# Attention scores as two products of rounded halves, four banks of queries and keys, and another order of side work

## The chip, the cores and the metric

The kernel runs on one core of a Trainium2 chip. The metric is the device time of one execution in microseconds (us), lower is better; it is read as the median of several runs. The engines are named as in the profile: PE (TensorE, matmuls; PEld are its weight loads), DVE (VectorE), ACT (ScalarE), POOL (GpSimd) and SP (SyncE, here only a queue of DMAs).

## What is computed

A batch of 8 sequences of 256 tokens with 128 features goes through four residual steps. The first one, which the change touches, is an attention with 16 heads, 16 features per head for queries and keys and 64 for values:

```
q, k, v = l2norm(q), l2norm(k), l2norm(v)
sim = einsum('bhid,bhjd->bhij', q, k)
attn = square(relu(sim))
out = tanh_norm(einsum('bhij,bhjd->bhid', attn, v))
x = x + out @ Wout
x = x + mixture_of_experts(layernorm(x))     # 32 experts of 64, top 8, and a shared one
x = x + sum_d softmax(W x + b)[d] * shifted(x, d)
x = x + mixture_of_experts(layernorm(x))     # the same weights
```

All tensors are float32, and the output must agree with a float32 reference. The norms of q, k and v are divided out behind the products (in the values' scales and in the output factors), so that the scores are made of unnormalised q and k.

## The kernel before

Everything is written out by hand: each engine has its own instruction list, and semaphores order them. There are two stages.

**Attention, `for b in range(B)`.** A batch b has four groups (slots of four heads), g = 0 to 3, numbered i = 4b + g over all. For each group PE makes `score(i)` (four banks S0), ACT `relu(i)`, DVE `squares(i)` (tile aT), PE `attend(i)` (bank O0) and ACT `keep_output(i)`. Between these stands other work. With n = b + 1 there is the preparation of the next batch: `transpose_tokens`, `pairs(n, t)` (q and k by token, for the norms), `values(n, t, k)` and `group(n, j)`, which makes q and k with features in rows, as score needs them. With q = b - 1 and r = b - 2 there is the finishing of earlier batches: `norms`, `transpose_norms`, `output_factors` (DVE), `transpose_factors`, `spread_factors`, `scale_output` (DVE, tile OTs) and `project(r, it)`, whose sum `add_attention` (DVE) adds to X.

**Three banks in rotation.** All of PE's side results go to banks 5, 6 and 7 in turn (W2, W0, W1). `attention_turns` writes the order of the jobs; a job can only start when the job three places ahead of it in that order has been read out (its `free_of` semaphore). The names of the jobs are xT (tokens), qk (pairs), v (values), g (groups), nb and nt (norms), ft and F (factors), y (project). In `group` a half bank is filled by one triple of products: x and the weights are each the sum of a rounded half and a low half (fp32r: one pass, where float32 takes two passes per recorded matmul and two records), and `split3` makes high by high, high by low and low by high. ACT's `keep_group` copies a group bank to the tile qk in float32, and that copy frees the bank.

**Expert weights.** The expert weights come in 32 pieces through six staging tiles (`STAGES`): SP loads a piece, ACT rounds it (`weight_high`, tile wfh), DVE makes the low half (`weight_low`, tile wfl). One piece goes in each of the 32 group steps, and the low halves of a batch are made in the batch behind it. SP's queue is in order, and a load of a piece waits for the low half made six pieces before.

**Experts, `for u in range(NU)`.** Eight units of 17 pairs each. PE makes `gate_up` and, four pairs later, `down`; ACT makes Silu and the rounded half, DVE two products, POOL the low half. In unit 0 the last batches' outputs are finished at fixed pairs p.

The order in which DVE works within a batch (before):

```
squares(NG * b + 3)
if more:
    value_norms(n, 1)
    clear_norms(n, 1)
if b:
    output_factors(q)
squares(NG * b + 4)
if n + 1 < B:
    tokens_low(n + 1)
```

Of the kernel before, what the change touches and what calls it, by code (L numbers as in the profile page):

```python
# [39 lines left out]
NQ = NG // 2 + 1  # L40
WQ_G, WK_G = (0, 1, 4, 5), (2, 3)
# [10 lines left out]
STAGES = 6  # L52
PC = WF // PIECES

# [28 lines left out]
def attention_turns(turns):  # L83
# [11 lines left out]
    for b in range(B):  # L95
        n, q, r = b + 1, b - 1, b - 2
        order += late(r, ("F", r, 2), ("F", r, 3)) + ([("pt", 0)] if b == B - 1 else [])
        order += coming(n, ("qk", n, 0), ("qk", n, 1), ("v", n, 0, 0), ("v", n, 0, 1)) + late(q, ("nb", q))
# [5 lines left out]
        order += coming(n, ("g", n, 0), ("g", n, 1), ("g", n, 2))  # L104
# [36 lines left out]

def up_banks():
# [16 lines left out]
def hybrid_layer(nc, x_in, wa_in, wo_in, wb_in, bb_in, gw_in, wf_in, sd_in, band, wdram, out):  # L159
# [4 lines left out]
    with ExitStack() as ctx:  # L164
# [9 lines left out]
        rowf = sb("rowf", [P, 1])  # L174
        sel = sb("sel", [P, 2, P], F32R)
# [36 lines left out]
        wTs = sb("wTs", [P, P])  # L212

# [3 lines left out]
        ld = Sems(ctx, nc, "in_x0 in_x in_wv0 in_wv1 in_wq in_wp in_wo in_wf0 in_wf1 in_wf2 in_wf3 in_wf4 in_wf5 in_sd in_gw in_wb in_bb zeroed")  # L217
        cs = Sems(ctx, nc, "id0 id half floors rid ind0 ind rm rf sel fpad zero sel1 sdz wah wal wph wpl wfh wfl sdh sdl")
        A = Sems(ctx, nc, "stats mv ve rstd xn xTh vraw sqv n2v n2q nm nm_v rr vi vc0 vc vp S relu a av Oc sqO "
# [20 lines left out]
        with ExitStack() as att:  # L240
# [10 lines left out]
            qk = ab("qk", [P, NQ, 2 * L])  # L251
# [143 lines left out]
        def _(pool):  # L395
# [126 lines left out]
            for u in range(NU):  # L522
                for p in range(NE if u < NU - 1 else NE - 1):
# [3 lines left out]
                    if u == 0 and p == 5:  # L527
                        last_output_norms(1)
                    if u == 0 and p == 6:
                        last_output_scales()  # L530
                    if p == (3 if u else 4) and u + 1 < NU:
# [7 lines left out]
        def _(act):  # L539
# [5 lines left out]

            first_weights_high(0)
# [111 lines left out]
            keep_group(0, 0)  # L658
            keep_group(0, 1)
            relu(0)  # L660
            tokens_high(1)
            for j in range(2, NQ):
                keep_group(0, j)
            for b in range(B):
# [14 lines left out]
                weight_high(NG * b)  # L679
# [7 lines left out]
                weight_high(NG * b + 1)  # L687
# [6 lines left out]
                if more:  # L694
                    square_values(n, 1)
                    keep_group(n, 0)
                    keep_group(n, 1)
                keep_output(NG * b + 2)
                if more:
                    keep_group(n, 2)  # L700
# [4 lines left out]
                weight_high(NG * b + 2)  # L705
# [4 lines left out]
                if last:  # L710
                    prep_normalise(1, range(CT // 2, CT))
# [4 lines left out]
                weight_high(NG * b + 3)  # L716
# [69 lines left out]
            for u in range(NU):  # L786
                first = u == 0
                for p in range(NP):
# [7 lines left out]
                    if first:  # L796
                        if p == 1:
                            keep_norms(B - 1)
                        if p == 8:
                            tanh_norms(B - 1)  # L800
                        if p == 11:
# [35 lines left out]
        def _(dve):  # L837
# [5 lines left out]
            dve.wait_ge(cs("rf"), 1)  # L843
            for m in range(HG):
# [38 lines left out]
            def clear_norms(n, t):  # L883
# [4 lines left out]
                v_.reciprocal(rr[:, n % 3, t, :], nm[:, n % 3, t, 0:2 * H]).then_inc(A("rr"), 1)  # L888

# [154 lines left out]
            normalise(1)  # L1044
            squares(0)
            tokens_low(1)
            first_scale_values()
            dve.wait_ge(cs("sel1"), 2)
            dve.wait_ge(cs("fpad"), 1)
            for b in range(B):  # L1050
# [20 lines left out]
                if b:  # L1071
                    if not last:
                        for k in range(NG * q, NG * b):
# [11 lines left out]
                if r >= 0:  # L1085
                    add_attention(r, 0)
                squares(NG * b + 3)
                if more:
                    value_norms(n, 1)
# [3 lines left out]

                squares(NG * b + 4)
                if n + 1 < B:
# [7 lines left out]
                if last:  # L1103
                    for k in range(NG * q, NG * b + 3):
# [76 lines left out]
            weight_low(NS - 1)  # L1181
            for u in range(NU):
                first = u == 0
                for p in range(NP):
# [3 lines left out]
                    if first:  # L1188
                        if p == 3:
                            gather_norms(B - 1)  # L1190
                        if p == 8:
                            output_factors(B - 1)
                        if p == 12:
                            scale_output(B - 1, 0)
                            scale_output(B - 1, 1)
                        if p == 14:
# [4 lines left out]
                        if p == 16:  # L1201
# [490 lines left out]
```

## Time and profile before

| | before |
|---|---|
| median of 3 runs | 548.19 us (547.99 to 548.92) |
| profiled execution | 546.98 us, of which the span is 545.2 us |
| instructions | 10298 |
| PE busy | 526.1 us (96%) |
| DVE busy | 421.7 us (77%) |
| ACT busy | 371.2 us (68%) |
| POOL busy | 332.5 us (61%) |
| granted TensorE clock | 0.999 of full speed |
| attention stage | from the start to about 215 us, some 26 us per batch |

The span is the time from the first to the last instruction of the profiled execution; its own time is 1.8 us more. Busy times are sums of recorded spans and say nothing of who waits for whom. That is read from the timeline of each engine: a start, a length, and in brackets the idle time ahead of an instruction and what ended it. Matmuls are pipelined, so that the next one starts before the one ahead is recorded as ended.

### The profile page before, as it was taken

What the parts mean: (1) busy time and instruction counts of PE and PEld (TensorE: products, weight loads), DVE (VectorE), ACT (ScalarE), POOL (GpSimd) and SP (SyncE); (2) the same over time, 40 slices, a digit from 0 to 9 for tenths busy, and PEclk for the clock granted to TensorE, in tenths of its full rate; (3) what the DMA queues carried; (4) which work ended last, traced back from release to release, by engine and by line L of the source; (5) the groups of instructions that cost most, each with busy time, mean ns of one, the idle gap of its engine ahead of it and who ended that gap; (6) DMA issues with size and microseconds to landing.
All of it is one profiled execution on the core that took longest, in us unless ns stands there. A gap on an engine that the chain in (4) does not pass through costs nothing.

```text
span 545.2 us, 10298 instructions
## 1 busy us (share of the span) xinstructions
PE 526.1 (96%) x3322; PEld 394.0 (72%) x3322; DVE 421.7 (77%) x1004; ACT 371.2 (68%) x682; POOL 332.5 (61%) x282
## 2 busy tenths in 40 slices
PE   7899899999999999998999999999999999999997
PEld 6565667676666666776778778778778877788884
DVE  5877888788979687669679679779778778777765
ACT  5697877686778876654555965965965965755654
POOL 6754938475865664484566656656655655666562
PEclk9999999999999999999999999999999999999999
DMA  7401010101010100850490940850860870761930
GB/s 222 131 2 31 1 32 1 32 0 32 1 31 1 31 2 21 189 122 1 107 208 7 222 116 5 207 132 6 197 141 7 194 163 5 181 149 42 220 74 20
DMA packets 37254, 44.77 MB, mean 82 GB/s; under 512 B 5840, under 2 KB 20304, under 8 KB 37200
## 3 DMA queue, kind: packets, MB, share of 16 engines
q1 hardware_dynamic: 32512, 42.40, 33.3%
q10 hardware_dynamic: 4688, 1.71, 1.3%
q8 instruction: 27, 0.44, 0.4%
q14 instruction: 27, 0.22, 0.2%
HBM read 40.94 MB, written 3.15 MB: 81 GB/s over the span
## 4 chain that ended last, share of the span: by engine, by line
PE 29%; POOL 12%; issue 9%; DVE 1%; DMA 1%; ACT 0%; POOLq 0%; DVEq 0%; SPq 0%; ACTq 0%
PE PS L1247 28%; POOL hl L519 10%; DMA wbc<-w_dram 1%; POOL mrstd L510 1%; POOL rstd L463 1%; DVE OTs L931 0%; PE PS L1534 0%; PE PS L1368 0%; DVE PS L1115 0%; DVE wsel L991 0%; POOL fxl L470 0%; PE PS L1555 0%; DVE hb L1120 0%; POOL mve L507 0%; DVE hl L1233 0%
## 5 line engine op out<-in xcount | busy, mean ns | idle before, releaser
L519 POOL TENSOR_TENSOR hl<-hb,hh 128x512 fp32r<-128x512 f32 x127 | 164.5, 1296 | 128.7 <-ACT hh L737 125.5
L730 ACT ACTIVATE sil<-PS 128x512 f32<-128x512 f32 (+1 forms) x136 | 80.8, 595 | 78.8 <-PE PS L1247 77.6
L1115 DVE TENSOR_TENSOR PS<-sil,PS 128x512 f32<-128x512 f32 x128 | 88.3, 690 | 53.0 <-PE PS L1247 32.3
L1247 PE MATMUL PS<-fxh,wfh 128*128 128x512 f32 x264 | 105.1, 398 | 2.5 <-DVE hb L1120 2.5
L737 ACT ACTIVATE hh<-hb 128x512 fp32r<-128x512 f32 x128 | 80.3, 627 | 35.1 <-DVE hb L1120 34.3
L1247 PE MATMUL PS<-fxl,wfh 128*128 128x512 f32 x264 | 104.2, 395 | 0.0
L1247 PE MATMUL PS<-fxh,wfl 128*128 128x512 f32 x264 | 103.8, 393 | 0.0
L1120 DVE TENSOR_TENSOR hb<-PS,wbc 128x512 f32<-128x512 f32 x128 | 88.5, 691 | 13.7 <-DMA wbc<-w_dram 6.4
L896 DVE SCALAR_TENSOR_TENSOR aT<-PS,rl 128x1024 f32<-128x1024 f32 x64 | 75.2, 1217 | 15.0 <-ACT rl L583 14.7
L583 ACT ACTIVATE rl<-PS 128x1024 f32<-128x1024 f32 x64 | 62.9, 1051 | 18.7 <-PE PS L1247 18.7
L438 POOL TENSOR_TENSOR sr<-n2o,half 128x32 f32<-128x32 f32 x7 | 37.9, 5413 | 44.3 <-DVE n2o L903 44.3
L1247 PE MATMUL PS<-aT,v 128*64 128x256 f32 x512 | 62.3, 385 | 0.6 <-POOL v L434 0.6
L1247 PEld LDWEIGHTS PS<-fxh,wfh 128*128 128x128 f32 x264 | 49.6, 188 | 15.8 <-DVE hb L1120 3.4
L1247 PEld LDWEIGHTS PS<-fxh,wfl 128*128 128x128 f32 x264 | 49.6, 188 | 11.9
L1247 PEld LDWEIGHTS PS<-fxl,wfh 128*128 128x128 f32 x264 | 49.6, 188 | 11.4
L1247 PE MATMUL PS<-hh,wfh 128*128 128x512 f32 x128 | 54.2, 424 | 1.0 <-DVE hl L1233 0.6
L1247 PE MATMUL PS<-hh,wfl 128*128 128x512 f32 x128 | 50.6, 396 | 0.0
L1247 PE MATMUL PS<-hl,wfh 128*128 128x512 f32 x128 | 50.5, 394 | 0.0
L1247 PEld LDWEIGHTS PS<-aT,v 128*64 128x64 f32 x512 | 34.0, 136 | 22.6 <-issue 5.6
L425 POOL TENSOR_TENSOR vi<-nm,half 128x16 f32<-128x16 f32 x14 | 40.5, 2894 | 9.8 <-DVE rr L888 9.8
L1247 PE MATMUL PS<-qk 32*128 32x256 f32 x512 | 37.5, 398 | 4.0 <-DVE aT L896 3.3
L1247 PEld LDWEIGHTS PS<-qk 32*128 32x128 f32 x512 | 24.4, 184 | 11.2 <-issue 7.1
(186 smaller groups left out, 899.6 us busy)
## 6 DMA issues: line engine op xcount, KB each, us to landing
wbc<-w_dram SPq DMA_DIRECT2D x48, 512.0 KB, 11.5
wbc<-w_dram SPq DMA_DIRECT2D x32, 128.0 KB, 3.0
wbc<-w_dram SPq DMA_DIRECT2D x16, 256.0 KB, 4.2
wfs<-wf_dram SPq DMA_DIRECT2D x32, 98.0 KB, 2.3
band_dram<-zero SPq DMA_DIRECT2D x16, 80.0 KB, 1.7
band<-band_dram ACTq DMA_DIRECT2D x4, 320.0 KB, 3.0
X<-x_dram SPq DMA_DIRECT2D x1, 896.0 KB, 8.0
Osb<-wa_dram SPq DMA_DIRECT2D x3, 256.0 KB, 3.8
```

The lines of the kernel that those rows point to most:

```text
L425: g.tensor_tensor(vi[:, t, :], nm[:, n % 3, t, 2 * H:3 * H], half[:, 1:2].to_broadcast([P, H]), ALU.pow).then_inc(A("vi"), 1)
L438: g.tensor_tensor(sr[:, :, :], n2o[:, :, :], half[:, 0:1].unsqueeze(2).to_broadcast([P, 2, H]), ALU.pow).then_inc(A("sr"), 1)
L463: g.tensor_tensor(rstd[:, :], ve[:, :], half[:, 1:2].to_broadcast([P, CT]), ALU.pow).then_inc(F("p_rstd"), 1)
L510: g.tensor_tensor(mrstd[:, :], mve[:, :], half[:, 1:2].to_broadcast([P, CT]), ALU.pow).then_inc(M("m_rstd"), 1)
L519: g.tensor_tensor(hl[:, n % RING, :], hb[:, n % RING, :], hh[:, n % RING, :].bitcast(F32), ALU.subtract).then_inc(F("hl"), 1)
L583: s.activation(rl[:, f, :, :], PS[:, S0 + 2 * f:S0 + 2 * f + 2, :], ACT.Relu).then_inc(A("relu"), 1)
L730: s.activation(sil[0:rows, n % 2, :], PS[0:rows, G0 + n % 2, :], ACT.Silu).then_inc(F("silu"), 1)
L737: s.activation(hh[:, n % RING, :], hb[:, n % RING, :], ACT.Copy).then_inc(F("hh"), 1)
L896: v_.scalar_tensor_tensor(aT[:, i % 2, 2 * f:2 * f + 2, :], PS[:, S0 + 2 * f:S0 + 2 * f + 2, :], 0.0, rl[:, f, :, :], ALU.max, ALU.mult).t ...
L1115: v_.tensor_tensor(PS[:, bank, :], sil[:, n % 2, :], PS[:, bank, :], ALU.mult).then_inc(F("t"), 1)
L1120: v_.tensor_tensor(hb[:, n % RING, :], PS[:, bank, :], wbc[u % 2][:, p, :], ALU.mult).then_inc(F("h"), 1)
L1247: return nc.tensor.matmul(o, w, m, start=start, stop=stop)
```

## The change

The float32 score product is replaced. `group` now makes four banks per batch: j = 0 holds the keys of groups 0 and 1, j = 1 their queries, j = 2 and 3 the same for groups 2 and 3. In each slot of 32 rows the 16 features of a head stand twice (the weights are laid out so). `group_high` (ACT) rounds a bank to fp32r, keys to kst, queries to qh. `group_low` (DVE) follows on the same bank and frees it: for queries it writes ql = q - qh; for keys it turns only the lower 16 rows of each slot into k - kh, by a column `low` that is 0 or -1. `score` makes two fp32r products that add up in the bank, kst by qh and kst by ql, which give (kh + kl)(qh + ql). Score waits for the two banks of its pair of groups to be free.

Beside that, `norms` stands ahead of the first `attend` of a batch; the pieces of the expert weights follow a table (none in batches 0 and 7, four in 1 and 6, six in 2 to 5) with seven stages; the last batches' outputs are finished one or two pairs earlier in unit 0; the filling transposes at the start of batch 0 are 4, not 10; and a Silu of one column stands first in ACT's list.

```
-NQ = NG // 2 + 1
-WQ_G, WK_G = (0, 1, 4, 5), (2, 3)
+NQ = NG
-STAGES = 6
+STAGES = 7
+PIECES_IN_SLOTS = ((0, 0, 0, 0), (1, 1, 1, 1), (1, 2, 1, 2), (1, 2, 1, 2), (1, 2, 1, 2), (1, 2, 1, 2), (1, 1, 1, 1), (0, 0, 0, 0))
...
-        order += coming(n, ("qk", n, 0), ("qk", n, 1), ("v", n, 0, 0), ("v", n, 0, 1)) + late(q, ("nb", q))
+        order += coming(n, ("qk", n, 0), ("qk", n, 1)) + late(q, ("nb", q)) + coming(n, ("v", n, 0, 0), ("v", n, 0, 1))
...
-        order += coming(n, ("g", n, 0), ("g", n, 1), ("g", n, 2))
+        order += [("g", n, j) for j in range(NQ)]
         order += coming(n + 1, ("xT", n + 1)) + late(q, ("ft", q)) + late(r, ("y", r, 1))
...
+            act.wait_ge(cs("half"), 2)
+            s.activation(unread[:, :], half[:, 0:1], ACT.Silu)
...
-            def keep_group(n, j):
+            def group_high(n, j):
                 act.wait_ge(*full("g", n, j))
-                after(act, A("S"), 2 * (NG * (n - 1) + (2 if j == 0 else NG)))
-                s.activation(qk[:, j, :], PS[:, bank_of("g", n, j), :], ACT.Copy).then_inc(free_of("g", n, j), 1)
+                after(act, A("S"), 2 * (NG * (n - 1) + (2 if j < 2 else NG)))
+                high = (qh if j % 2 else kst)[:, j // 2, :]
+                s.activation(high, PS[:, bank_of("g", n, j), :], ACT.Copy).then_inc(A("gh"), 1)
...
+            def group_low(n, j):
+                dve.wait_ge(A("gh"), NQ * n + j + 1)
+                x, k = PS[:, bank_of("g", n, j), :], j // 2
+                if j % 2:
+                    v_.tensor_tensor(ql[:, k, :], x, qh[:, k, :].bitcast(F32), ALU.subtract).then_inc(free_of("g", n, j), 1)
+                else:
+                    v_.scalar_tensor_tensor(kst[:, k, :], kst[:, k, :].bitcast(F32), low[:, 0:1], x, ALU.mult,
+                                            ALU.add).then_inc(free_of("g", n, j), 1)
...
                 squares(NG * b + 3)
                 if more:
+                    group_low(n, 0)
+                    group_low(n, 1)
                     value_norms(n, 1)
                     clear_norms(n, 1)
                 if b:
                     output_factors(q)
 
+                if more:
+                    group_low(n, 2)
                 squares(NG * b + 4)
+                if more:
+                    group_low(n, 3)
...
-                pe.wait_ge(*freed("g", b, jq))
-                pe.wait_ge(*freed("g", b, 1))
+                c = g % 2 * L
+                pe.wait_ge(*freed("g", b, g // 2 * 2))
+                pe.wait_ge(*freed("g", b, g // 2 * 2 + 1))
                 after(pe, A("a"), 2 * i)
                 for jt in range(2):
-                    for s in range(HG):
-                        rows = slice(SLOT * s, SLOT * (s + 1))
-                        last = mm(PS[:, S0 + s, jt * L:(jt + 1) * L], qk[rows, 1, k0 + jt * P:k0 + (jt + 1) * P],
-                                  qk[rows, jq, q0:q0 + L], True, True)
...
+                    for part, queries in enumerate((qh, ql)):
+                        for s in range(HG):
+                            rows = slice(SLOT * s, SLOT * (s + 1))
+                            last = mm(PS[:, S0 + s, jt * L:(jt + 1) * L], kst[rows, g // 2, c + jt * P:c + (jt + 1) * P],
+                                      queries[rows, g // 2, c:c + L], part == 0, part == 1)
...
-                    fill_idle(10 if b == 0 else 8, "qk", n, 0)
+                    fill_idle(4 if b == 0 else 8, "qk", n, 0)
...
+                if b:
+                    norms(q)
                 attend(NG * b)
...
                     group(n, 2)
+                    group(n, 3)
```

**Where DVE's instructions go.** Before, in batch 2, DVE's list from the squares of the third group (aT) to the low half of the next tokens (xTl) reads as follows; nmx to Fpad are `output_factors`:

```order
L896 SCALAR_TENSOR_TENSOR aT<-PS,rl 128x1024 [waits av,relu] x2
L875 TENSOR_REDUCE n<-sqv 128x16 [waits sqv]
L886 TENSOR_REDUCE nm<-n 128x48 [waits n2q,n2v]
L888 RECIPROCAL rr<-nm 128x32 [waits nm]
L908 TENSOR_REDUCE nmx<-nn 128x32 [waits n]
L910 RECIPROCAL rec<-nmx 128x32 [waits nmx]
L912 TENSOR_TENSOR f<-rec,rr 128x32 [waits rec]
L915 TENSOR_TENSOR ff<-f,th 128x32 [waits th,f1]
L922 CAST Fpad<-ff 128x8x4 [waits full6,ff]
L924 TENSOR_TENSOR Fpad<-ff,Fpad 128x8x4 [waits fhi]
L896 SCALAR_TENSOR_TENSOR aT<-PS,rl 128x1024 [waits av,relu] x2
L868 TENSOR_TENSOR xTl<-PS,xTh 128x256 [waits xTh]
```

In the changed kernel the same place begins with two of the four new instructions (kst and ql are what `group_low` writes),

```order
L933 SCALAR_TENSOR_TENSOR aT<-PS,rl 128x1024 [waits av,relu] x2
L924 SCALAR_TENSOR_TENSOR kst<-kst,low,PS 128x512 [waits gh]
L922 TENSOR_TENSOR ql<-PS,qh 128x512 [waits gh]
L903 TENSOR_REDUCE n<-sqv 128x16 [waits sqv]
L914 TENSOR_REDUCE nm<-n 128x48 [waits n2q,n2v]
```

and ends, behind the same `output_factors`, with the other two around the squares of the fourth:

```order
L961 TENSOR_TENSOR Fpad<-ff,Fpad 128x8x4 [waits fhi]
L924 SCALAR_TENSOR_TENSOR kst<-kst,low,PS 128x512 [waits gh]
L933 SCALAR_TENSOR_TENSOR aT<-PS,rl 128x1024 [waits av,relu] x2
L922 TENSOR_TENSOR ql<-PS,qh 128x512 [waits gh]
L896 TENSOR_TENSOR xTl<-PS,xTh 128x256 [waits xTh]
```

So three new instructions stand between the two squares, and the fourth, which frees the last group bank, stands behind the second squares.

**What PE waits for.** Before, PE's list in batch 3 from the third group bank (first row) over the last score (qk), the next tokens (xnA) and the factors' transposition (Fpad) to the second `project` (wout) is this; the third group bank and `project` share bank 5 (free5):

```order
L1247 MATMUL PS<-xTh,wah 128x256 [waits free5]
...
L1247 MATMUL PS<-qk 128x256 [waits a,free7,free6]
L1247 MATMUL PS<-qk 128x256 x7
L1267 MATMUL PS<-ident,xnA 128x128 [waits free6,xn]
L1267 MATMUL PS<-ident,xnA 128x128
...
L1340 MATMUL PS<-ident,Fpad 128x128 [waits free7,f]
L1340 MATMUL PS<-ident,Fpad 128x128
L1247 MATMUL PS<-wout,OTs 128x128 [waits free5,free7,free6]
```

In the changed kernel, same batch, the fourth group bank (first row) and `project` (last row) share bank 5, with nothing on that bank in between:

```order
L1297 MATMUL PS<-xTh,wah 128x256 [waits free5]
...
L1297 MATMUL PS<-qh,kst 128x256 [waits a,free6,free5]
...
L1317 MATMUL PS<-ident,xnA 128x128 [waits free6,xn]
...
L1391 MATMUL PS<-ident,Fpad 128x128 [waits free7,f]
...
L1297 MATMUL PS<-wout,OTs 128x128 [waits free7,free6,free5]
```

Before, that bank was read out by one ACT copy; now `project` stands behind the `group_low` that DVE has behind its squares.

**The start.** Before, DVE's list ahead of the first squares is

```order
L875 TENSOR_REDUCE n<-sqv 128x16 [waits sqv]
L1016 TENSOR_REDUCE nm<-n 128x16 [waits n2v]
L863 TENSOR_SCALAR xnA<-X,mvA,rsA 128x128 [waits full6,rstd]
L863 TENSOR_SCALAR xnA<-X,mvA,rsA 128x128
L896 SCALAR_TENSOR_TENSOR aT<-PS,rl 128x1024 [waits relu] x2
```

and in the changed kernel

```order
L903 TENSOR_REDUCE n<-sqv 128x16 [waits sqv]
L1053 TENSOR_REDUCE nm<-n 128x16 [waits n2v]
L891 TENSOR_SCALAR xnA<-X,mvA,rsA 128x128 [waits full6,rstd]
L891 TENSOR_SCALAR xnA<-X,mvA,rsA 128x128
L924 SCALAR_TENSOR_TENSOR kst<-kst,low,PS 128x512 [waits gh,low]
L922 TENSOR_TENSOR ql<-PS,qh 128x512 [waits gh]
L933 SCALAR_TENSOR_TENSOR aT<-PS,rl 128x1024 [waits relu] x2
```

The first score, on PE, now stands behind the first kst and ql of this list.

## Rows read from the trace of the kernel before

**Rows 1.** The page: busy time, and the granted clock in 40 slices.

```profile
PE 526.1 (96%) x3322; PEld 394.0 (72%) x3322; DVE 421.7 (77%) x1004; ACT 371.2 (68%) x682; POOL 332.5 (61%) x282
PEclk9999999999999999999999999999999999999999
```

**Rows 2.** Busy time in batch 4: window, then PE, PEld, DVE, ACT, POOL.

```profile
120.00:146.00 26.00, 25.77 (x228) 17.72 (x230) 22.20 (x49) 20.02 (x36) 17.16 (x13) 1.00 0.07 17
```

**Rows 3.** PE timeline of batch 4: start, length, line, tiles, count.

```profile
118.52 0.39 PE L1247 MATMUL PS<-FT,sel 32*128 32x256 f32 x2
133.48 1.15 PE L1247 MATMUL PS<-qk 32*128 32x256 f32 x16
...
134.90 0.28 PE L1247 MATMUL PS<-xTh,wal 128*128 128x256 f32 x1
...
135.97 0.28 PE L1247 MATMUL PS<-xTh,wal 128*128 128x256 f32 x1
...
138.97 1.15 PE L1247 MATMUL PS<-qk 32*128 32x256 f32 x16
140.05 0.44 PE L1267 MATMUL PS<-ident,xnA 128*128 128x128 f32 x2
...
142.57 1.95 PE L1247 MATMUL PS<-wout,OTs 128*128 128x128 f32 x16
144.45 0.39 PE L1247 MATMUL PS<-FT,sel 32*128 32x256 f32 x2
```

**Rows 4.** DVE timeline of batch 4.

```profile
119.06 2.63 DVE L931 TENSOR_TENSOR OTs<-Osb,PS 128x512 f32<-128x512 f32 x4
...
135.18 0.38 DVE L954 BATCH_NORM_AGGREGATE mv<-stats 128x2 f32<-128x6 f32 x4
...
135.72 2.36 DVE L896 SCALAR_TENSOR_TENSOR aT<-PS,rl 128x1024 f32<-128x1024 f32 x2
...
141.30 2.36 DVE L896 SCALAR_TENSOR_TENSOR aT<-PS,rl 128x1024 f32<-128x1024 f32 x2
143.57 0.41 DVE L868 TENSOR_TENSOR xTl<-PS,xTh 128x256 fp32r<-128x256 f32 x1
```

**Rows 5.** ACT timeline of batch 4: the third and fourth relu.

```profile
134.66 1.94 ACT L583 ACTIVATE rl<-PS 128x1024 f32<-128x1024 f32 x2 [0.94 <-PE PS L1247]
...
140.19 1.99 ACT L583 ACTIVATE rl<-PS 128x1024 f32<-128x1024 f32 x2
```

**Rows 6.** Tile qk from 113.0 to 114.2 us: durations in ns, first and last start.

```profile
L1247 PEld LDWEIGHTS PS<-qk x16: 181/184/185, 113.0 to 113.6; 32*128 32x128 f32 x16
L1247 PE MATMUL PS<-qk x16: 374/374/478, 113.0 to 113.8; 32*128 32x256 f32 x16
```

**Rows 7.** PE and DVE timelines of the start and of batches 1 and 2.

```profile
15.19 1.15 PE L1247 MATMUL PS<-qk 32*128 32x256 f32 x16 [0.61 <-ACT qk L575]
16.81 0.59 DVE L863 TENSOR_SCALAR xnA<-X,mvA,rsA 128x128 f32<-128x128 f32 x2
17.42 2.36 DVE L896 SCALAR_TENSOR_TENSOR aT<-PS,rl 128x1024 f32<-128x1024 f32 x2
...
19.92 1.15 PE L1247 MATMUL PS<-qk 32*128 32x256 f32 x16 [0.93 <-DVE aT L896]
...
41.91 1.15 PE L1247 MATMUL PS<-qk 32*128 32x256 f32 x16 [0.53 <-DVE aT L896]
...
65.83 1.10 PE L1247 MATMUL PS<-qk 32*128 32x256 f32 x13 [0.76 <-DVE aT L896]
```

**Rows 8.** ACT, PE and SP timelines where the experts begin.

```profile
215.10 1.82 SPq L361 DMA_DIRECT2D w_dram<-wTs  x4
216.29 0.37 ACT L613 ACTIVATE wfh<-wfs 128x196 fp32r<-128x196 f32 x1 [4.09 <-DMA wfs<-wf_dram]
...
217.74 0.51 PE L1247 MATMUL PS<-FT,sel 32*128 32x256 f32 x4 [1.27 <-ACT FT L605]
...
218.93 1.28 ACT L730 ACT_TABLE_LOAD   x1
...
223.22 0.50 PE L1247 MATMUL PS<-fxh,wfh 128*128 128x512 f32 x1 [1.08 <-DVE hb L1120]
...
247.85 0.50 PE L1247 MATMUL PS<-fxh,wfh 128*128 128x512 f32 x1 [1.42 <-DVE hb L1120]
```

More of the change, by code:

```diff
@@ L139, in expert_turns, with pieces_in @@
             turns.add(MB, "pc", u + 1)
+def pieces_in(b, slots=range(NG)):
+    first = sum(sum(PIECES_IN_SLOTS[c]) for c in range(b))
+    a = first + sum(PIECES_IN_SLOTS[b][:slots[0]])
+    return range(a, a + sum(PIECES_IN_SLOTS[b][k] for k in slots))
 def up_banks():
@@ L174, in hybrid_layer @@
         rowf = sb("rowf", [P, 1])
+        rowh = sb("rowh", [P, 1], I32)
+        rowg = sb("rowg", [P, 1])
+        low = sb("low", [P, 1])
         sel = sb("sel", [P, 2, P], F32R)
@@ L678, in _ @@
                     keep_norms(q)
-                weight_high(NG * b)
+                for k in pieces_in(b, [0]):
+                    weight_high(k)
                 relu(NG * b + 2)
@@ L686, in _ @@
                 keep_output(NG * b + 1)
-                weight_high(NG * b + 1)
+                for k in pieces_in(b, [1]):
+                    weight_high(k)
                 if b == B - 2:
@@ L704, in _ @@
                     tanh_norms(q)
-                weight_high(NG * b + 2)
+                for k in pieces_in(b, [2]):
+                    weight_high(k)
+                if last:
+                    prep_normalise(1, range(CT // 2, CT))
                 relu(NG * b + 4)
@@ L715, in _ @@
                     keep_factors(q)
-                weight_high(NG * b + 3)
+                for k in pieces_in(b, [3]):
+                    weight_high(k)
                 if b == 0:
@@ L843, in _ @@
             dve.wait_ge(cs("rf"), 1)
+            v_.tensor_scalar(rowh[:, :], rowid[:, :], DK, None, ALU.bitwise_and).then_inc(cs("rh"), 1)
+            dve.wait_ge(cs("rh"), 1)
+            v_.tensor_copy(rowg[:, :], rowh[:, :]).then_inc(cs("rg"), 1)
+            dve.wait_ge(cs("rg"), 1)
+            v_.tensor_scalar(low[:, :], rowg[:, :], -1.0 / DK, None, ALU.mult).then_inc(cs("low"), 1)
             for m in range(HG):
@@ L1044, in _ @@
             normalise(1)
+            dve.wait_ge(cs("low"), 1)
+            group_low(0, 0)
+            group_low(0, 1)
             squares(0)
             tokens_low(1)
+            group_low(0, 2)
+            group_low(0, 3)
             first_scale_values()
@@ L1072, in _ @@
                     if not last:
-                        for k in range(NG * q, NG * b):
+                        for k in pieces_in(q, [0, 1]):
                             weight_low(k)
@@ L1086, in _ @@
                     add_attention(r, 0)
+                if b and not last:
+                    for k in pieces_in(q, [2, 3]):
+                        weight_low(k)
                 squares(NG * b + 3)
                 if more:
+                    group_low(n, 0)
+                    group_low(n, 1)
                     value_norms(n, 1)
@@ L1103, in _ @@
                 if last:
-                    for k in range(NG * q, NG * b + 3):
+                    for k in pieces_in(q):
                         weight_low(k)
@@ L1440, in _ @@
                     values(n, 0, 1)
-                if b:
-                    norms(q)
                 score(NG * b + 2)
```

62 lines of the change are left out of this document (32 added, 30 removed).

## Prediction, made before the changed kernel ran

> **What bounds the kernel now.** I read the page first: PE is busy 526.1 of 545.2 us at the full clock in all 40 slices [rows 1], and the reader is to see that only PE time, or a new wait of PE, can count. Then busy time by batch: in 26 us of batch 4 PE works 25.77, DVE 22.20, ACT 20.02 [rows 2]. So PE bounds a batch, but DVE has under 4 us to spare. Then the timelines of PE and DVE side by side in batch 4, for where those 4 us lie. PE's batch runs from 118.52 to 144.45, 25.93 us [rows 3]. DVE's spare time is not where the change adds work: from the squares at 135.72 over the squares at 141.30 to their end at 143.57 DVE has no idle bracket [rows 4]. Last the start and the passage to the experts, the two places where PE does wait: for DVE at the start [rows 7], and at 217.74, 223.22 and 247.85 [rows 8].
>
> **The score product.** A score's 16 recorded matmuls start in 0.8 us, four waves for four row groups, and PE goes on at 140.05 where the score began at 138.97: 1.08 us [rows 3, 6]. A wave is 256 columns in two passes; with the next start 1.08 us later I put 4 x 0.213 = 0.85 for the waves (my reading of the 0.8 us from first to last start) and 0.23 fixed. The new one has four waves of one pass. In `group` fp32r matmuls of 256 columns start (135.97 - 134.90) / 9 = 0.119 us apart, with a new weight load each [rows 3]. So a score takes 0.48 + 0.23 = 0.71, 0.37 less; 32 of them, 12 us of PE. Bounds: nothing, if 16 weight loads took as long as the old product; 0.43 (half of 0.85) at best. I take 0.37, since the row with loads is the nearest.
>
> The Trainium skill speaks against it: TensorE: Matmul & The Clock Gate, section LDWEIGHTS, says that a load takes its columns by 1.2 GHz, no matter how few rows. For 128 columns that is an estimate of 0.107 us, and 16 in a line would be 1.7 us, a score slower than now. The row has 16 loads starting within 0.6 us [rows 6], so loads of four row groups run side by side; the trace decides.
>
> **The fourth group bank.** Six more matmuls at 0.119: 0.72 us of PE per batch, 8 times; one more ACT copy (0.55). PE's own work per batch falls by 4 x 0.37 - 0.72 = 0.76 us.
>
> **The four new DVE instructions.** The trace has no instruction like them on group banks; the nearest reads a PSUM bank and a tile of 512 columns: four in 2.63 us, 0.66 each [rows 4]. I take 0.64; bounds 0.55 and 0.70. That is 2.6 us per batch, and six weight pieces for four add 0.6: 22.2 becomes 25.4 of DVE work against 25.2 of PE. This already leaves no room, and the order decides more than the sum.
>
> **The walk from the third score of a batch (time 0).** Before: relu starts at 1.18 [rows 5], the squares at 2.24, the fourth squares at 7.82 to 10.09, `project` at 9.09 (142.57 - 133.48) [rows 3, 4]. After: the score ends 0.37 earlier, so squares at 1.87. Between the two squares three `group_low` come in: 7.82 - 0.37 + 3 x 0.64 = 9.37; the squares' 2.27 take it to 11.64, the fourth `group_low` to 12.3. `project` shares its bank with the fourth group bank, so it waits for that. PE itself would be there at 9.09 - 2 x 0.37 + 0.72 = 9.07. A stall of **3.2 us**, where there was none. The relu is no help: 6.71 less 0.37 plus one more copy 0.55, so it is there before the squares. Queued behind `project` on PE are the spreading of factors and the next batch's first score; DVE waits in turn for the factors and then has its idle time there.
>
> The first half of the batch (118.52 to 133.48, 14.96) can give back little: two scores, 0.74, of which some 0.45 goes to a bank of the values that now waits for ACT's copy of the norms, and the pairs still wait for DVE's second product. I take 0.3 saved. Per batch: +3.2 - 0.02 - 0.3 = **+2.9**. This holds for batches 2 to 5. In batch 4 the statistics that end at 135.56 [rows 4] leave 0.2 us ahead of the squares, where two or three weight pieces at 0.3 now come too: +0.6. Sum of the four: +12.2.
>
> **Batch 6** has no tokens to come, so the rotation gives `project` the third bank, and only the router's logits wait for the fourth: +1.0. **Batch 7** has three scores and no group: PE could save 1.1; DVE holds the first one, I take -0.8.
>
> **The start.** The first score began at 15.19 behind an ACT copy; now it stands behind DVE's normalisation, which ends at 17.40, and two `group_low`: 18.7 [rows 7]. Its squares ran 17.42 to 19.69; now relu comes 1.7 behind the score's start, so 20.4 to 22.7; the low half of tokens 0.4 and a third `group_low` 0.64 let the filling go at 23.75, and the second score comes at 24.2 for 19.92, +4.3. In batch 0 ACT has no weight pieces and PE's later waits absorb 1.5 of it. Batch 1 meets the same chain as above, with the filling and the next score in place of `project` behind the fourth bank (65.83 before [rows 7]): +2.2. Sum for the first two batches **+5.0**, bounds +3 and +7.
>
> **The passage to the experts.** ACT waited 4.09 us there for a weight piece that hung in SP's queue, and PE 1.27 us for factors behind it; SP's store of the expert factors (215.10) hung there too; the Silu table took 1.28 at 218.93 [rows 8]. With the pieces done before batch 7 and the table loaded at the start, where ACT waits for its first DMA, PE's wait of 1.27 goes. That of 1.08 at 223.22 stays in part, since the pair behind it needs DVE's first hidden product, which stands behind DVE's four factor products. With the table's delay out I take -1.7. The wait of 1.42 at 247.85 stood behind `output_factors` and the router in one pair; they are apart now: -1.4. Bounds of the two: -1 and -4. The seventh stage and `norms` ahead of `attend` I cost at nothing: the load is hidden by a batch's distance, and `norms` only changes place.
>
> **Sum.** +5.0 + 12.2 + 1.0 - 0.8 - 3.1 = +14.3 on the profiled 546.98: 561.3. The median of the runs shown is 1.2 more, so **562.4** on it.
>
> **Rivals.**
> 1. *The chain is looser (half the stall).* If DVE's instructions overlap more than the rows show, or the third score comes earlier against DVE, the stall is 1 to 2 us a batch and the start +2 to +3. At 1.5: (1.5 - 0.3) x 4 + 0.6 + 2.5 + 0.5 - 3.9 = +4.5, 552.7. For it: DVE's idle time in a batch is real; against it: it lies elsewhere.
> 2. *PE stays the bound (faster).* One mechanism: `group_low` of the fourth bank is off PE's path, since what stands on that bank does not hold `project`. Then seven batches save 0.76 and batch 7 0.8, the passage 3.1, and the start costs what its chain costs, about +2: 548.2 - 5.3 - 0.8 - 3.1 + 2 = 541.0. It decides once the fourth bank is free 9.1 us behind the third score. Four free instructions would bring it to 12.3 - 2.6 = 9.7, so a low price for them alone is not enough; the squares ahead of it would have to end earlier too. The order of the banks speaks against it.
> 3. *The clock falls in the stalls.* The trace has no idle time of PE above 1.5 us behind the start and no slice below the full clock [rows 1]. A wait of 3.2 us per batch and one of 4 us at the start are new. If the 3 us of work behind each ran at half speed: 5 x 3 = 15 us more, 577. The page named above says in its section on oscillation that idle gaps send the clock back to half; by it the sum would be this one.
> 4. *The new product saves nothing* (loads in line): +0.37 x 32 less what the stalls cover (the scores ahead of a stall of DVE): some +6, 568.
>
> **Chances.** The walk as it stands, with its error, 553 to 567: 0.56. Rival 1: 0.12. Rival 2: 0.17. Rival 3: 0.06. Rival 4: 0.05. Within 0.2%, which is about what a measurement of this kernel can tell from no change, 0.04. So faster 0.17, same 0.04, slower 0.79. The predicted time is that of the walk. The range goes from 542, into rival 2, to 570, over rival 4; left out are the lower half of rival 2 and rival 3. The walk's own range is 553 to 567.
>
> **What the profile will show.** Right: in batches 2 to 5 a PE wait of about 3 us at wout, with DVE's ql as what ended it; a batch of 28.8 us; DVE without idle time from the third squares to ql; scores 0.7 us apart from what follows; the second score near 24 us; ACT's wait for a weight piece gone. Wrong: a batch under 26 us, or PE waits that end on ACT; new DVE instructions under 0.5 us; a score slot still of 1.08; or a granted clock below 0.98.

## The result, and the profile after

The changed kernel takes 574.88 us (median of 4 runs, 572.89 to 575.23) against 548.56 us (4 runs, 547.99 to 550.62): a ratio of 1.047, 95% interval 1.044 to 1.050. It is slower. The forecast of slower was right; the time of 562.4 us is 12.5 us short, and the range (542 to 570) does not hold the result. The profiled execution took 574.87 us, of which the span is 573.1, 27.9 more than before.

The page of the kernel after, busy time and the granted clock in 40 slices:

```profile
PE 533.8 (93%) x3364; PEld 403.8 (70%) x3364; DVE 441.5 (77%) x1039; ACT 375.7 (66%) x690; POOL 332.1 (58%) x282
PEclk9799999898989899999999999999999999999999
```

Against [rows 1] PE is busy 7.7 us *more*, though its scores are shorter, and the clock row, flat before, has dents in slice 2 and in every second one from 8 to 14. A page that shows more busy time for less work says: look at the clock. Next the batches 2 to 6 by windows (window, its length, then PE, PEld, DVE, ACT, POOL, and the clock as a share of full speed):

```profile
74.81:105.57 30.76, 26.43 (x235) 18.94 (x234) 23.18 (x43) 21.12 (x38) 16.60 (x10) 0.96 0.06 15
105.57:135.91 30.34, 26.53 (x235) 19.06 (x234) 24.02 (x46) 21.05 (x38) 16.60 (x10) 0.95 0.09 21
135.91:166.59 30.68, 26.90 (x235) 19.23 (x234) 24.95 (x54) 21.09 (x38) 18.35 (x14) 0.95 0.08 21
166.59:196.56 29.97, 26.36 (x235) 18.90 (x235) 24.02 (x46) 22.49 (x42) 16.60 (x10) 0.96 0.09 21
196.56:226.12 29.56, 27.88 (x245) 19.82 (x244) 23.97 (x48) 21.29 (x37) 15.97 (x9) 0.91 0.05 12
```

A batch of 25.93 [rows 3] has become 30.0 to 30.8. PE timeline of batch 3, from the third score to the next batch:

```profile
120.55 0.39 PE L1297 MATMUL PS<-qh,kst 32*128 32x256 f32 x4
...
121.22 0.39 PE L1297 MATMUL PS<-xTh,wah 128*128 128x256 f32 x1
...
127.74 1.68 PE L1297 MATMUL PS<-aT,v 128*64 128x256 f32 x14
130.04 0.41 PE L1391 MATMUL PS<-ident,Fpad 128*128 128x128 f32 x2 [0.62 <-DVE kst L924]
132.90 3.06 PE L1297 MATMUL PS<-wout,OTs 128*128 128x128 f32 x16 [2.45 <-DVE ql L922]
135.89 0.58 PE L1297 MATMUL PS<-FT,sel 32*128 32x256 f32 x2
...
137.56 0.50 PE L1297 MATMUL PS<-FT,sel 32*128 32x256 f32 x4 [0.17 <-DVE OTs L968]
```

Three things are to be seen. The score's slot is 121.22 - 120.55 = 0.67 us, for 1.08 before [rows 3]. Ahead of `project` PE stands still twice, 0.62 and 2.45, together 3.07, both ended by an instruction of `group_low`. And `project` itself now takes 3.06 us for 16 matmuls that took 1.95. DVE's timeline of the same stretch says why PE waits:

```profile
122.38 2.36 DVE L933 SCALAR_TENSOR_TENSOR aT<-PS,rl 128x1024 f32<-128x1024 f32 x2 [0.62 <-ACT rl L600]
124.73 0.75 DVE L924 SCALAR_TENSOR_TENSOR kst<-kst,low,PS 128x512 fp32r<-128x512 f32 x1
125.39 0.68 DVE L922 TENSOR_TENSOR ql<-PS,qh 128x512 fp32r<-128x512 f32 x1
125.99 1.21 DVE L903 TENSOR_REDUCE n<-sqv 128x16 f32<-128x1024 f32 x1
...
129.16 0.74 DVE L924 SCALAR_TENSOR_TENSOR kst<-kst,low,PS 128x512 fp32r<-128x512 f32 x1
129.81 2.35 DVE L933 SCALAR_TENSOR_TENSOR aT<-PS,rl 128x1024 f32<-128x1024 f32 x2
132.08 0.68 DVE L922 TENSOR_TENSOR ql<-PS,qh 128x512 fp32r<-128x512 f32 x1
```

No idle bracket from the third squares to the last `ql`: DVE is the chain. And the windows of PE over the same time say why `project` is long:

```profile
129.00:133.00 4.00, 0.93 (x7) 1.00 0.00 0
133.00:134.00 1.00, 1.00 (x8) 0.83 0.00 0
134.00:135.00 1.00, 1.00 (x7) 0.50 0.08 16
135.00:136.00 1.00, 1.00 (x9) 0.50 0.00 0
136.00:137.00 1.00, 1.00 (x18) 0.50 0.00 0
137.00:138.00 1.00, 0.83 (x12) 0.96 0.00 0
```

The clock is still full during the wait and falls to 0.50, the lower of the two levels (1.2 GHz), when PE has just gone back to work; it stays there for some 3.5 us. So the stall is paid once as idle time and again in the work behind it. The same happens behind each of the four stalls at the ends of batches 2 to 5, and behind the last one it lasts twice as long, from 195.1 to 201.9 us, most of it in batch 6:

```profile
196.00:201.00 5.00, 4.98 (x32) 0.50 0.00 0
202.00:207.00 5.00, 5.00 (x54) 1.00 0.12 25
```

The Trainium skill (TensorE: Matmul & The Clock Gate, section HAM oscillation) says that idle gaps send the clock back to half; here the trace agrees, though the gap was broken by a pair of transposes of 0.41 us.

The start, PE and then DVE:

```profile
19.46 0.39 PE L1297 MATMUL PS<-qh,kst 32*128 32x256 f32 x4 [3.50 <-DVE ql L922]
...
25.79 0.58 PE L1297 MATMUL PS<-qh,kst 32*128 32x256 f32 x4
...
15.62 1.16 DVE L903 TENSOR_REDUCE n<-sqv 128x16 f32<-128x1024 f32 x1
...
18.63 0.68 DVE L922 TENSOR_TENSOR ql<-PS,qh 128x512 fp32r<-128x512 f32 x1
```

The first score begins 4.3 us later than before [rows 7], and PE then runs at 0.50 from 21 to 31 us.

### The profile page after: what moved, and what is told of

It is laid out like the page before. It is cut to its first block, busy times and chain, and to the rows that moved or that the text cites. A ratio compares the mean times of both kernels' runs of the same rounds, so it can differ in the third digit from the quotient of the medians.

```text
span 573.1 us, 10433 instructions
## 1 busy us (share of the span) xinstructions
PE 533.8 (93%) x3364; PEld 403.8 (70%) x3364; DVE 441.5 (77%) x1039; ACT 375.7 (66%) x690; POOL 332.1 (58%) x282
## 4 chain that ended last, share of the span: by engine, by line
PE 46%; issue 17%; POOL 17%; DVE 14%; ACT 5%; DMA 1%; SPq 0%; POOLq 0%; DVEq 0%; ACTq 0%
PE PS L1297 44%; POOL hl L533 13%; DVE aT L933 5%; ACT rl L600 2%; DVE ql L922 2%; DVE n L903 2%; ACT v L574 1%; DMA Osb<-wa_dram 1%; DVE kst L924 1%; DVE OTs L968 1%; POOL rstd L477 1%; POOL mrstd L524 1%; ACT sqO L610 1%; POOL vi L488 1%; POOL wal L495 0%
## 5 line engine op out<-in xcount | busy, mean ns | idle before, releaser
L1297 PE MATMUL PS<-wout,OTs 128*128 128x128 f32 x256 | 35.8, 300 | 10.1 <-DVE ql L922 9.8
L1297 PEld LDWEIGHTS PS<-wout,OTs 128*128 128x128 f32 x256 | 33.5, 210 | 13.4 <-issue 13.1
```

The lines of the kernel that those rows point to most:

```text
L1297: return nc.tensor.matmul(o, w, m, start=start, stop=stop)
```

## Experiments

The kernels of experiments 1 to 4 ran on one chip, those of 5 to 8 on another, each time beside runs of the kernel before (medians 548.58 and 548.54 us).

**1. The fourth bank's release.** `group_low(n, 3)` is moved ahead of the batch's last squares.

```
                 if more:
                     group_low(n, 2)
-                squares(NG * b + 4)
-                if more:
                     group_low(n, 3)
+                squares(NG * b + 4)
```

> The changed kernel (574.9 us) with one move: in each batch the group_low of the fourth bank stands ahead of the fourth squares on DVE, not behind them. Theory A (PE's wait of 2.45 us at the second project is for that bank alone, and the half clock behind it is its consequence): the bank is free 2.3 us earlier, project starts about 130.5 where it was 132.9, the wait shrinks to some 0.2 us, the clock stays at full, and what is late next is the low half of the tokens, which frees the bank of the factors: a batch of 27.5 to 28 us for 30.4, -2.8 us in each of batches 2 to 5 and about -2 for the others together: 561 to 563. Rival B (DVE's total work sets the batch, the order within it does not): no more than 2 us of gain, 573 to 575. Rival C (the clock falls for another reason): the wait goes but the clock still falls, 565 to 568.

Measured 559.69 us (559.3 to 562.69), ratio 1.023 (1.019 to 1.026): 15.2 us of the 26.3 lost are back by the change of places of two DVE jobs, a little more than I expected (561 to 563). PE timeline:

```profile
152.34 0.41 PE L1390 MATMUL PS<-ident,Fpad 128*128 128x128 f32 x2 [0.61 <-DVE kst L924]
...
152.94 2.02 PE L1296 MATMUL PS<-wout,OTs 128*128 128x128 f32 x16 [0.19 <-DVE ql L922]
155.49 0.39 PE L1296 MATMUL PS<-FT,sel 32*128 32x256 f32 x2 [0.52 <-issue]
```

The 2.45 has become 0.19, and `project` takes 2.02 again. A batch is 27.3 us long (152.94 to 180.26 from `project` to `project`). The theory of the late bank holds. The 15.2 us hold both prices of the stall, the idle time and the half clock behind it; experiment 2 takes them apart.

**2. The same stall without the idle PE.** In batches 2 to 5 PE waits for the squares of the output and then does 14 transposes that nobody reads, into a free bank, ahead of `project`. DVE's chain is untouched.

```
                 if last_batch:
                     prep_combine(0)
+                if 2 <= b < B - 2:
+                    pe.wait_ge(A("sqO"), NG * b + 4)
+                    keep_busy(14)
                 project(r, 1)
```

> The changed kernel with 14 transpositions of the identity into the output bank (as soon as ACT has copied it) ahead of the second project of batches 2 to 5. They change no data and no wait; they only fill PE's idle time, from about 131.3 us in the profiled batch, where ACT's squares of the output end at 130.6. Theory A (PE's idle time itself brings the half clock): project takes 1.95 us again instead of 3.06, and with the spreads and the score behind it a batch is 1.5 to 2 us shorter; four batches and the cold first half of batch 6: -6 to -8, 567 to 569. Rival C (the clock falls by something else, as DVE's load or a fixed time): no change, or longer by what the filling delays, 574.9 to 577.

Measured 568.96 us (568.45 to 569.52), ratio 1.038 (1.036 to 1.040): 5.9 us less than the changed kernel from 56 useless transposes, 1.5 us for each of the four stalls.

```profile
130.04 1.75 PE L1441 MATMUL PS<-ident 128*128 128x128 f32 x14 [0.18 <-ACT sqO L610]
132.31 2.02 PE L1297 MATMUL PS<-wout,OTs 128*128 128x128 f32 x16 [0.52 <-DVE ql L922]
```

`ql` still ends the wait at the same place in DVE's order, but `project` runs in 2.02 instead of 3.06, and from batch 3 on the clock is full (PE by windows, batches 3 to 5 and batch 6):

```profile
105.26:192.66 87.40, 80.94 (x741) 1.00 0.09 22
192.66:220.49 27.83, 25.65 (x246) 1.00 0.05 12
```

This tells the two prices of a stall apart: the clock's share was 1.5 us, beside 3.07 of idle time. The two profiles bear it out. From the stalled `project` of batch 2 to that of batch 6 the changed kernel takes 120.50 us (102.38 to 222.88) and this one 113.96 (103.29 to 217.25), 6.5 us for four stalls: 1.3 to 1.5 for each of the first three and 2.4 for the last, behind which the half clock lasts longest.

**3. The side edits alone,** with the old product: `norms` ahead of the first `attend`, the table of pieces with its seventh stage, Silu at the start, the last outputs earlier.

```
                 if b:
                     norms(q)
                 attend(NG * b)
                 ...
-                weight_high(NG * b)
+                for k in pieces_in(b, [0]):
+                    weight_high(k)
```

> The kernel before with the side edits of the change alone: the table of weight pieces with seven stages, norms ahead of the first attend (with its turn of the banks), the Silu at the start, the last outputs' earlier places; the score product, the three group banks and 10 filling transpositions stay. Theory A: this part of the change is a gain, and all of the loss is the new product's: the passage to the experts shortens by 1.5 to 3 us and the batches by nothing: 545.5 to 547. Rival D (six pieces in batches 2 to 5 or the seventh stage load ACT and DVE so that PE waits there too): 548.5 to 552.

Measured 544.42 us (544.0 to 544.89), ratio 0.993 (0.991 to 0.995). This beats both kernels, and by more than I expected (545.5 to 547). The side edits are worth -4.2 us, so the rest of the change, the product with its fourth bank and its four filling transposes in place of ten, costs 30.5.

**4. Half of the low parts left out.** No `ql`: ACT's rounding frees the banks of queries, and the second product takes qh again, so that TensorE's work stays. The kernel leaves out the low half of the queries.

```
+                signal = free_of("g", n, j) if j % 2 else A("gh")
...
                 if j % 2:
-                    v_.tensor_tensor(ql[:, k, :], x, qh[:, k, :].bitcast(F32), ALU.subtract).then_inc(free_of("g", n, j), 1)
+                    return
...
-                    for part, queries in enumerate((qh, ql)):
+                    for part, queries in enumerate((qh, qh)):
```

> The changed kernel without the low half of the queries: group_low for the two banks of queries is left out, ACT's rounding frees those banks, and the second product of a score takes the rounded queries again (so the scores are those of other numbers). PE's work is the same. Theory A (it is the DVE queue ahead of the fourth bank's release): PE's waits for ql go, project starts at PE's own pace, the next wait is the tokens' low half about 1.3 us earlier than now; a batch of 26.3 to 27 us, with the start 0.7 us earlier and warm after it: 548 to 555. Rival B (DVE's total work decides): two instructions of 0.66 us less per batch, 1.3 us a batch: 563 to 566.

Measured 554.48 us (553.58 to 555.99), ratio 1.012 (1.009 to 1.014), within the expected 548 to 555: two DVE instructions of 0.6 less per batch, with the fourth bank free before the squares. Since the bank comes early and the work is less at once, this run alone does not part the two; against experiment 1, where the bank is early too, the less work is worth 5.2 us.

**5. No low parts at all.** ACT frees all four banks and both low halves are left out. It is what the product would give if the low halves cost nothing.

```
-                s.activation(high, PS[:, bank_of("g", n, j), :], ACT.Copy).then_inc(A("gh"), 1)
+                s.activation(high, PS[:, bank_of("g", n, j), :], ACT.Copy).then_inc(free_of("g", n, j), 1)
...
             def group_low(n, j):
+                return
...
-                    for part, queries in enumerate((qh, ql)):
+                    for part, queries in enumerate((qh, qh)):
```

> The changed kernel without any group_low: ScalarE's rounding frees all four banks, keys stay rounded in all 32 rows, the second product takes the rounded queries again; leaves out both low halves, TensorE does all the same matmuls. It is what the new product would give if the low halves cost nothing. Theory (four score slots of 0.68 in place of 1.08 a batch, -1.6, and one more group of 0.84; no late release): 0.5 to 0.8 us a batch below the kernel with the side edits alone (544.4), so 538 to 542, score(1) near 20 us and no wait at the project. Rival, that the product by itself costs on TensorE or on ScalarE (a fourth rounding of 0.7 us late for its bank): 545 or more, with waits on relu's or the factors' lines in the first half of a batch.

Measured 543.28 us (541.77 to 543.56), ratio 0.990 (0.987 to 0.992). That is only 1.1 us below the side edits alone (544.42, on the other chip), outside the 538 to 542 that I expected. PE timeline of a batch, its only waits:

```profile
143.29 0.50 PE L1298 MATMUL PS<-FT,sel 32*128 32x256 f32 x4 [0.40 <-DVE OTs L969]
...
150.95 0.50 PE L1298 MATMUL PS<-wah,xTh 128*128 128x512 f32 x1 [0.29 <-ACT n2T L616]
```

A batch lasts 25.59 us (`project` at 129.06 and 154.65), with the side edits alone 25.69 (131.80 and 157.49). PE works 0.8 less, and 0.69 of it goes into these two waits, which did not exist while the score took 1.08. So even a free product was worth 0.1 us a batch: PE was near enough to its suppliers that shorter scores mostly uncovered them.

**6. The start.** The kernel of experiment 1, and in the start the first two low halves ahead of the value norms and the normalisation.

```
             normalise(0)
+            group_low(0, 0)
+            group_low(0, 1)
             value_norms(0, 1)
             first_value_floor(1)
             normalise(1)
-            group_low(0, 0)
-            group_low(0, 1)
```

> The kernel with the low half of the fourth bank ahead of the squares (559.7, ratio 1.023), and in the start also the first two low halves ahead of the value norms of the first tile. Theory (score(1) waits on VectorE's line, 3.5 us at 19.5 us and then a half clock till 31 us): the first scores come about 2 us earlier, at 17.5, and the first queue behind them with them; expected 1 to 3 us below, 556.7 to 558.7. Rival, that the value norms and the scaled values are then late by the same 2 us and the first attend waits instead: within 0.5 of 559.7, with the wait moved to the first attend or the first values.

Measured 557.51 us (557.32 to 561.4), ratio 1.018 (1.015 to 1.021), 2.2 below experiment 1 and within the expected 556.7 to 558.7. PE timeline:

```profile
16.94 0.51 PE L1296 MATMUL PS<-qh,kst 32*128 32x256 f32 x4 [2.17 <-DVE ql L922]
...
23.41 0.39 PE L1296 MATMUL PS<-qh,kst 32*128 32x256 f32 x4
```

The second score comes 1.9 us earlier than in experiment 1 (25.31), and the scaled values were not missed.

**7 and 8. The side edits in two parts,** on the kernel before: the pieces' table with the seventh stage, and the rest.

```
 7: -                weight_high(NG * b)
    +                for k in pieces_in(b, [0]):
    +                    weight_high(k)
 8: +                if b:
    +                    norms(q)
                     attend(NG * b)
    ...
    +            s.activation(unread[:, :], half[:, 0:1], ACT.Silu)
    ...
    -                        if p == 8:
    +                        if p == 6:
                                 output_factors(B - 1)
```

> The kernel before with one side edit alone: the table of weight pieces with its seventh stage; old product, norms where they were, no Silu at the start. Question: where does the gain of the side edits together (548.6 to 544.4) come from? Theory pieces: ScalarE's 4.09 us wait for a weight piece at 216.29 and SyncE's stuck queue behind it go, and with them the 1.27 us wait for the first experts' tokens; expected -1.5 to -2.5, 546.0 to 547.1, with the 1.42 us wait at unit 0's last outputs still there. Rival, that the whole gain lies in the order of the last outputs and the norms: 548.2 to 549, and the other run of this call has all of it.

> The kernel before with the other side edits: norms ahead of the batch's first attend, one Silu at the start, the last outputs earlier in unit 0; the old table of weight pieces with six stages. Theory (each side edit pays its own wait): the 1.42 us wait at 247.85 goes, and part of the 1.3 us table load at the passage; expected -1.4 to -2.7, 545.9 to 547.2, the 1.27 us wait still there. Together with the run of the pieces this should sum to -4.1 of the kernel with all side edits. Rival, that the gains overlap (one wait removed uncovers the next): each alone gives under 1 us, 547.6 or more.

Measured: pieces 544.76 us (543.41 to 545.98), ratio 0.994 (0.991 to 0.996); rest 544.25 us (543.74 to 546.5), ratio 0.993 (0.990 to 0.995). Each is better than expected, and the two do not add up: -3.8 and -4.3, but -4.2 together. The PE timelines, of the pieces first, then of the rest:

```profile
216.41 0.50 PE L1262 MATMUL PS<-FT,sel 32*128 32x256 f32 x4
...
246.29 0.50 PE L1262 MATMUL PS<-fxh,wfh 128*128 128x512 f32 x1 [1.42 <-DVE hb L1136]
```

```profile
216.73 0.50 PE L1250 MATMUL PS<-FT,sel 32*128 32x256 f32 x4 [1.20 <-ACT FT L608]
...
242.28 0.50 PE L1250 MATMUL PS<-fxh,wfh 128*128 128x512 f32 x1 [1.00 <-DVE hb L1123]
```

As waits they are where they should be: the pieces remove the wait of 1.27 at the passage and leave that of 1.42; the rest leaves 1.20 and cuts 1.42 to 1.00. The rest also makes each batch 0.24 shorter (167.37 - 141.67 = 25.70 from `project` to `project`, before 168.51 - 142.57 = 25.94). Up to unit 0's last `project` the profiled executions of pieces, rest and both stand 1.6, 3.2 and 3.8 us ahead of before. Two things blur the rest of the way. In the one with both the clock fell once, behind waits that the rest alone has too (windows of PE, of both and then of the rest alone):

```profile
68.00:70.00 2.00, 1.98 (x7) 0.50 0.00 0
70.00:72.00 2.00, 2.00 (x19) 0.67 0.03 8
```

```profile
68.00:70.00 2.00, 1.91 (x14) 1.00 0.00 0
70.00:72.00 2.00, 2.00 (x27) 1.00 0.00 0
```

And the experts' matmuls ran at another pace (last section). Whether pieces and rest overlap by more than that stays open; no run here tests it.

## Why the prediction was right, and where it failed

The sum was +14.3 us on the profiled execution; the span grew by 27.9. By its own steps (batch starts on PE: before 65.83, 170.42, 197.04 and unit 0 at 214.8; after 74.81, 196.56, 226.12 and 244.1):

| step | predicted | measured |
|---|---|---|
| start and batches 0, 1 | +5.0 | +9.0 |
| batches 2 to 5 | +12.2 | +17.2 |
| batch 6 | +1.0 | +2.9 |
| batch 7 | -0.8 | +0.2 |
| passage and experts | -3.1 | -1.4 |

- **The score product: right.** Slot 0.71 predicted, 0.67 measured. The trace decided against the rule on weight loads that the prediction names (the Trainium skill, TensorE: Matmul & The Clock Gate, section LDWEIGHTS): by it a score had to be slower than 1.08. The same page of the Trainium skill, in its section The mechanism under packing small matmuls, says that a weight load overlaps with matmuls of other row groups, and by that sentence the trace agrees.
- **Group_low: right.** 0.64 predicted, 0.60 to 0.66 from start to start. DVE's work in a batch came to 23.2 to 25.0 us, 25.0 in batch 4, for which I had 25.4.
- **The walk: right.** Third score to `project` 12.3 predicted, 132.90 - 120.55 = 12.35 measured; stall 3.2 predicted, 0.62 + 2.45 = 3.07 measured, ended by `ql` as named. Experiment 1 shows that the place of one instruction behind the squares is what makes it. Where the clock stays full, the batch is the one forecast: batches 3 to 5 of experiment 2 take 29.02, 29.35 and 29.03 us, for 28.8, 29.4 and 28.8 by the walk. In the changed kernel they take 30.34, 30.68 and 29.97.
- **The failed step: the clock, put outside the sum.** I wrote rival 3, "The clock falls in the stalls", worked out its price (5 x 3 us), gave it 0.06, and let the sum and the range go by a full clock. The reason was that "the trace has no idle time of PE above 1.5 us behind the start": true, and no evidence, since the stall that I had just derived was twice as long. The clock did fall, at every stall of batches 2 to 5 and at the start; the mean of 0.976 is below the 0.98 that I had named as a sign of being wrong. Its price is less than I feared: 1.5 us a stall (experiment 2), and half speed for 3.5 us can't cost PE more than 1.8. Of the 6.5 us that the four stalls cost so in the profiles, 1.7 fall in batch 6 (29.56 against 27.83 in experiment 2). With the rest the four batches come to 12.2 + 4.8 = 17.0, measured 17.2.
- **The start: undersized by 4.0 us, in part by the same step.** The first score came at 19.46, 18.7 predicted, and the second at 25.79, 24.2 predicted. From there to batch 1 (48.99) PE took 23.20 us. Before it took 21.99, and I had put it 1.5 shorter, since later waits of PE would absorb so much: they did not. About 5.3 us of this stretch, up to 31, ran at half clock, which can have cost up to 2.7. In the profile of experiment 2, the same code up to there with less time at half clock, the stretch takes 22.28. No run here has the changed start at a full clock, so how much is the clock's and how much the missing absorption stays open. The wait itself is real too: experiment 6 gives 2.2 us back by DVE's order alone.
- **Batch 6:** at a full clock (experiment 2) it takes 27.83, 1.2 more than before, for 1.0 predicted. In the changed kernel the stall at the end of batch 5 leaves it at 0.91 of the clock, 1.7 us more; the same omission.
- **Batch 7:** -0.8 predicted, +0.2 measured. PE waits there for OTs (0.39 and 0.44) and for the copied norms (0.78), where before it had one wait of 0.43. I had none of these in the sum.
- **The first half of a batch: right, and hidden by the clock.** 0.3 saved was predicted. In the changed kernel nothing is seen (105.57 to 120.55 is 14.98, before 14.96), but its first 0.8 us run at half clock. With the clock full the same stretch takes 14.69 (experiment 2, 105.26 to 119.95).
- **The passage: right in direction, half the size.** -3.1 predicted, -1.4 measured in the changed kernel. The wait of 1.27 went as forecast and that of 1.08 stayed in part (0.82), but the one of 1.42 did not go, 0.76 of it is left (at 270.73): 2.2 less in these three. And at 472.95 PE waits 0.92 for ACT's Silu, which before has no match. The -4.2 of experiment 3 is not the passage alone: the batches are in it, where I had costed `norms` ahead of `attend` at nothing, and the rest of the side edits makes a batch 0.24 shorter (experiment 8).
- **Rival 2** asked whether an off-path fourth bank would make the kernel faster. It does not: with the bank early the kernel is still at 559.7 and a batch at 27.3, for 25.7 with the side edits alone, since the low halves still cost DVE time at other places of the chain. Only without any of that work (experiment 5) is it below before.

From the changed kernel down: the fourth bank's place 15.2, its share of the half clock included; the start 2.2; all low halves as DVE work 14.2 (557.51 to 543.28, with the half clock that is left in the start of experiment 6). What is left, 1.1 us, is all that the new product had to offer.

## What to carry to other kernels

When your own walk yields a new idle time of PE of some microseconds in each round, the clock belongs in the sum, not among the rivals: price the work behind the stall at the lower level, and take the absence of such a row in the old trace as "not seen", not as "does not happen". When an engine with less than four free microseconds a round gets new work, first ask which buffer that work frees, and put it ahead of anything long that nobody waits for as urgently; two instructions swapped were worth 15 us here, the clock included. And before you shorten work on the bound engine, look how near its suppliers are: four scores each 0.4 us shorter, with a fourth bank to fill, took 0.8 us of PE's work out of a batch and gave 0.1, even with the low halves free.

## What the runs showed of the hardware that I had not expected

**The same waits cost the clock in one execution and not in another.** The waits of 0.45, 0.83 and 0.83 us between 62 and 69 us stand alike in the profiles of experiments 3 and 8; in one the clock fell to 0.50 for some 3 us, in the other not. So it was with the stall at the end of batch 1: PE waits 0.72 and 2.36 us there in the profiles of the changed kernel and of experiment 2, by the same code; in the first the clock stayed full, in the second it was at 0.50 from 73 to 80 us. The runs of one kernel differ likewise: experiment 8's five runs at a mean clock of 0.999 or 1.000 took 543.74 to 544.46 us, the one at 0.995 took 546.5; experiment 1's run at 0.982 took 562.69, those at 0.990 to 0.994 took 559.3 to 559.99.

**The pace of the same matmuls differs between profiles at a granted clock of 1.00.** In the experts three 128x512 products follow three others after 0.693 us in the profiles of experiments 7 and 8, and after 0.697 to 0.698 in that of before and all the others (means over some 130 such gaps). The chip is not what tells them apart, since experiments 5 and 6 ran on the same one as 7 and 8. Each kernel has one profile, so whether the pace goes with the kernel or with the execution stays open. Over the 285 us of the experts it is an estimated 1.8 us, nearly half of what the side edits gain; a few tenths of a per cent can't be read from two profiles.

**A small DVE instruction was held up by a GpSimd one.** In the changed kernel a difference of 64x128, 0.28 us long in the trace of before, took 1.72; DVE, then POOL:

```profile
49.70 1.72 DVE L1150 TENSOR_TENSOR wfl<-sdr,wfh 64x128 fp32r<-64x128 f32 x1
```

```profile
49.37 1.91 POOL L448 TENSOR_TENSOR v<-v,vc 128x1024 f32<-128x1024 f32 x1
```

It ends 0.14 us behind the POOL instruction that had begun before it. All ten profiles of this case bear on it. In four (the changed kernel, experiments 1, 2 and 6) the DVE instruction starts 0.33 us behind the POOL one and takes 1.72. In the six others it starts no later than the POOL one and takes 0.27 or 0.28; where both start at once it is POOL that takes longer, 2.05 for 1.91 (experiment 4):

```profile
47.63 0.27 DVE L1151 TENSOR_TENSOR wfl<-sdr,wfh 64x128 fp32r<-64x128 f32 x1
```

```profile
47.63 2.05 POOL L448 TENSOR_TENSOR v<-v,vc 128x1024 f32<-128x1024 f32 x1
```

The Trainium skill (SBUF — State Buffer, section SBUF: two separate sides) says that a DVE instruction with two SBUF inputs waits for a GpSimd one that holds the port pair for its whole length; the ten profiles agree with that. That the GpSimd one can be held as well is seen in one row only, the 2.05. No run here was made to test either.
